# Cross-attention and ternary feed-forward kernel: output product by halves of the rows, value product by pairs of heads, and statistics taken up one step later

## The reference

```
x = x + attention(layernorm(x), ctx)      # x: 64 x 512 x 512, ctx: 64 x 77 x 512
x = x + ffn(layernorm(x))

attention: q = x Wq (16 heads of 32, in 4 groups), k = ctx Wk, v = ctx Wv (4 heads)
    q, k = rope(q), rope(k); sum over the 4 groups of q (the einsum sums over g)
    p = softmax(q k / sqrt(32)) per head over the 77 rows of ctx
    out = mean over heads of (p v); return out @ Wo        # 32 x 512
ffn: w = sign(weight) where |weight| > 0.5 mean|weight|; input quantised by max|x| / 127
    return (round(x / s) @ w.T) * w_scale * s + bias
```

## Time and profile before

| | |
|---|---|
| median of 3 runs | 1268.88 us (1268.54 to 1269.37) |
| the profiled execution | 1268.9 us, its span 1267.0 us |
| TensorE busy, of the span | 1201.2 us, 95% (weight loads 983.0, 78%) |
| VectorE | 1124.7 us, 89% |
| ScalarE | 1001.1 us, 79% |
| GpSimd | 794.2 us, 63% |
| granted TensorE clock, mean | 0.991 |
| DMA | 205 GB/s over the span |

### The profile page before, as it was taken

How to read it: one execution, slowest core, us unless ns; L and a number is a source line. 1 busy time by engine, 2 the same in 40 slices (tenths; PEclk the granted TensorE clock), 3 DMA queues, 4 the chain that set the end, 5 groups by cost and what they waited for, 6 DMA issues and landing times.

```text
span 1267.0 us, 42077 instructions
## 1 busy us (share of the span) xinstructions
PE 1201.2 (95%) x12408; PEld 983.0 (78%) x12471; DVE 1124.7 (89%) x2410; ACT 1001.1 (79%) x2339; POOL 794.2 (63%) x1536
## 2 busy tenths in 40 slices
PE   7999999999999999999999999999789999999997
PEld 7998888888888888888888888888645555555554
DVE  4656999999999999999999999999878888888887
ACT  4566888888888888888888888888768888888886
POOL 4767898898998988989989889899700000000000
PEclk9999999999999999999999999999889999999999
DMA  9772555555555555555555543323029999999945
GB/s 291 225 205 66 160 178 169 173 173 170 164 178 166 178 168 175 170 174 162 182 163 181 164 123 94 87 84 84 2 99 398 403 396 398 399 408 396 395 206 212
DMA packets 97241, 260.26 MB, mean 205 GB/s; under 512 B 42538, under 2 KB 53994, under 8 KB 76723
## 3 DMA queue, kind: packets, MB, share of 16 engines
q1 hardware_dynamic: 97154, 259.75, 59.6%
q10 hardware_dynamic: 48, 0.07, 0.0%
HBM read 137.11 MB, written 122.64 MB: 205 GB/s over the span
## 4 chain that ended last, share of the span: by engine, by line
DVE 44%; PE 35%; issue 15%; DVEq 3%; ACT 1%; POOL 1%; DMA 0%; SPq 0%; POOLq 0%; ACTq 0%
DVE amax L903 10%; PE pT_ps L1265 10%; PE sc_ps L1265 9%; DVE x_sb L940 8%; DVE mx_sb L918 7%; DVE bn_sb L930 6%; DVE e_sb L922 6%; PE qo_ps L1069 5%; PE xT_ps L1256 5%; DVE bn_sb L910 3%; PE sc_ps L1263 2%; DVE mv_sb L947 2%; DVE rinv_sb L890 2%; PE xT_ps L1058 1%; PE pT_ps L1263 1%
## 5 line engine op out<-in xcount | busy, mean ns | idle before, releaser
L1210 PE MATMUL qo_ps<-wqs,xT_sb 128*128 128x128 f32 x2048 | 262.6, 281 | 0.9 <-ACT xT_sb L700 0.9
L1210 PEld LDWEIGHTS qo_ps<-wqs,xT_sb 128*128 128x128 f32 x2048 | 238.2, 191 | 21.5 <-issue 20.0
L1233 PEld LDWEIGHTS pT_ps<-v_blk,pT_sb 103*128 103x128 f32 x1536 | 197.3, 190 | 11.8 <-ACT pT_sb L712 0.9
L940 DVE SCALAR_TENSOR_TENSOR x_sb<-x_sb,mv_sb,xT_ps 128x512 f32 (+1 forms) x256 | 180.0, 745 | 25.5 <-DVE bn_sb L930 10.8
L1233 PE MATMUL pT_ps<-v_blk,pT_sb 103*128 103x136 f32 x1536 | 200.1, 280 | 0.3 <-ACT pT_sb L712 0.3
L1008 DVE TENSOR_TENSOR x_sb<-x_sb 128x512 f32 (+1 forms) x256 | 164.7, 684 | 1.2 <-ACT x_sb L758 1.2
L700 ACT ACTIVATE xT_sb<-xT_ps 128x512 f32<-128x512 f32 x256 | 139.1, 595 | 33.3 <-PE xT_ps L1136 28.9
L663 ACT ACTIVATE sq_sb<-x_sb 128x512 bf16 (+1 forms) x256 | 162.4, 634 | 0.6 <-DVE x_sb L940 0.2
L903 DVE TENSOR_REDUCE amax<-x_sb (+1 forms) x128 | 154.6, 1208 | 0.3 <-issue 0.3
L758 ACT ACTIVATE x_sb<-pT_ps,mean,cols 128x512 f32<-128x512 f32 x128 | 99.5, 777 | 63.6 <-PE pT_ps L1265 63.6
L1265 PE MATMUL pT_ps<-wT,x_sb 128*128 128x512 f16 x512 | 131.4, 379 | 3.2
(11 more groups left out here) (135 smaller groups left out, 2673.7 us busy)
## 6 DMA issues: line engine op xcount, KB each, us to landing
out_y<-x_sb SPq DMA_DIRECT2D x112, 1024.0 KB, 6.5
x_sb<-in_x SPq DMA_DIRECT2D x128, 512.0 KB, 3.9
x_sb<-out_y SPq DMA_DIRECT2D x48, 1024.0 KB, 8.9
x_sb<-in_ctx SPq DMA_DIRECT2D x38, 256.0 KB, 4.0
k_blk<-k_scr SPq DMA_DIRECT2D x256, 9.6 KB, 1.7
v_scr<-x_sb SPq DMA_DIRECT2D x38, 68.0 KB, 3.0
k_scr<-x_sb SPq DMA_DIRECT2D x38, 64.0 KB, 3.3
v_blk<-v_scr SPq DMA_DIRECT2D x128, 10.2 KB
```

Source lines behind the costliest of these rows:

```text
L940: dve.scalar_tensor_tensor(out=x1_at(kj, gj, t), in0=x_sb[:, kj // 2, 2 * (kj % 2) + t, :], scalar=mv_sb[:, kj, t, 0:1], in1=bank[t][:, :] ...
L1210: last = pe.matmul(bank[2][:, t * HD:(t + 1) * HD], xT_sb[:, t, c, :], wqs[:, c, :], start=c == 0, stop=c == EC - 1)
L1233: last = pe.matmul(bank[6][:, t * HEADS * VC:(t + 1) * HEADS * VC], pT_sb[0:CR, t, c * P:(c + 1) * P], v_blk[0:CR, slot, c, :, :].rearrang ...
```

## The change

- **Output product.** GpSimd writes `os_sb` with rounded and rest of each tile once (2 x 64 columns for both tiles instead of 2 x 128). One pair of 64-row transposes turns it: the transposed first tile stands in partitions 0 to 63, the second in 64 to 127. `wst` now holds rounded weights and rest side by side, on all partitions. The product is four matmuls over 64 rows and 512 columns: rounded weights for either tile, then the rest for either tile, accumulated. Each tile has its own bank.
- **Banks.** The output product has a tensor of its own, `y_ps`. q goes to bank 0, where x transposes also go, so these now wait for `q_copied` of the step before. The transposes of q and of `os_sb` go into free columns of the scores' banks and wait for `sub_done_t`; the score matmuls wait for both their copies.
- **Order on TensorE.** The output product stands ahead of q instead of behind it.
- **Chunks.** A transpose of probabilities takes 128 columns (chunks overlap), and the value matmul contracts over 128 rows, but only over the 68 columns of two neighbouring heads, chunk c with heads c and c+1.
- **Statistics.** `bn_sb` has two buffers. `bn_aggr` and the variance of a pair follow a step after its `bn_stats`.
- **Order on the others.** VectorE: see the rows below. ScalarE copies q behind the exponentials. GpSimd puts the two powers between operations that wait for each other.

The core of the diff:

```diff
-STARTS = [c * CR if (c + 1) * CR <= SC else SC - CR for c in range(CHUNKS)]
+STARTS = [min(c * CR, SC - P) for c in range(CHUNKS)]
...
-            then(dve.tensor_copy(wst[:, :], woc[:, :]))
-            then(dve.tensor_tensor(wst[2 * D:4 * D, :], woc[2 * D:4 * D, :],
-                                   wst[2 * D:4 * D, :].bitcast(F32), ALU.subtract))
+            then(dve.tensor_copy(wst[:, 0, :], woc[:, :]))
+            then(dve.tensor_tensor(wst[:, 1, :], woc[:, :], wst[:, 0, :].bitcast(F32), ALU.subtract))
...
-                    pool.tensor_tensor(ost_sb[:, :, :, 0, :],
-                                       pw2_sb[:, :, 0, 0:D].unsqueeze(2).broadcast_to([P, 2, 2, D]),
-                                       pw2_sb[:, :, 1, 0:D].unsqueeze(2).broadcast_to([P, 2, 2, D]),
-                                       ALU.add).then_inc(o_ready, 1)
+                    pool.tensor_tensor(os_sb[:, :, 0, :], pw2_sb[:, :, 0, 0:D], pw2_sb[:, :, 1, 0:D],
+                                       ALU.add).then_inc(o_ready, 1)
...
+                    pool.tensor_tensor(os_sb[:, :, 1, :], o_sb[:, :, 0:D], os_sb[:, :, 0, :].bitcast(F32),
+                                       ALU.subtract).then_inc(os_ready, 1)
...
-                    act.activation(oT_sb[:, :, :].rearrange("p c (h r) -> p c h r", h=2), rows_of(qo_ps, P, 2),
+                    act.activation(oT_sb[:, :].rearrange("p (c h r) -> p c h r", c=1, h=2), rows_of(sc_ps, SC + P, 1),
...
-                    held(ost_ready, j + 1, ost_count, 1)
-                    for t in range(2):
-                        last = halves(qo_ps, P + t * HALF,
-                                      ost_sb[:, t, :, :, :].rearrange("p a b d -> p (a b d)").bitcast(F32))
-                    last.then_inc(oT_done, 1)
+                    held(os_ready, j + 1, o_count, 1)
+                    halves(sc_ps, SC + P, os_sb[:, :, :, :].rearrange("p t a d -> p (t a d)").bitcast(F32))\
+                        .then_inc(oT_done, 1)
...
-                    if isinstance(j, int) and j <= RESID:
-                        at_least(pe, xT_copied_t, 2 * j)
-                    else:
-                        held(added_t, 2 * (j - RESID), added_count, 2)
+                    if not isinstance(j, int) or j > 0:
+                        held(q_copied, j, q_count, 1)
...
-                            last = halves(pT_ps, (t * CHUNKS + c) * HALF, e_sb[:, kj % 2, t, start:start + CR])
+                            last = halves(pT_ps, (t * CHUNKS + c) * HALF, e_sb[:, kj % 2, t, start:start + P])
...
-                    at_least(pe, sub_done_t, 2 * j)
+                    if resid:
+                        pe.wait_ge(oT_copied, resid[0] + 1)
...
+                    for w in range(2):
+                        for t in range(2):
+                            rows = slice(t * HALF, (t + 1) * HALF)
+                            last = pe.matmul(y_ps[:, t, :], oT_sb[rows, :], wst[rows, w, :], start=w == 0, stop=w == 1)
+                    last.then_inc(y_done, 1)
...
-                    for t in range(2):
-                        pe.matmul(bank[t][:, :], oT_sb[:, t, :], wst[:, :], start=True, stop=True)\
-                          .then_inc(y_done_t, 1)
...
-                        for c in range(CHUNKS):
-                            last = pe.matmul(bank[6][:, t * HEADS * VC:(t + 1) * HEADS * VC],
-                                             pT_sb[0:CR, t, c * P:(c + 1) * P],
-                                             v_blk[0:CR, slot, c, :, :].rearrange("p h d -> p (h d)"),
-                                             start=c == 0, stop=c == CHUNKS - 1)
+                        for c in (0, 2, 1):
+
+
+                            at0 = (t * HEADS + c) * VC
+                            last = pe.matmul(bank[6][:, at0:at0 + 2 * VC], pT_sb[:, t, c * P:(c + 1) * P],
+                                             v_blk[:, slot, c, c:c + 2, :].rearrange("p h d -> p (h d)"),
+                                             start=c == 0, stop=c == 1)
```

More of the change, by code:

```diff
@@ L169, in build @@
         wqs = sb("wqs", [P, EC, HD])
-        wst = sb("wst", [P, E], F32R)
+        wst = sb("wst", [P, 2, E], F32R)
         wbar = sb("wbar", [P, D])
@@ L730, in step @@
                                        scale=rs_sb[:, kj, t:t + 1]).then_inc(exp_done_t, 1)
+                if proj:
+                    j, kj, gj = proj
+                    act.wait_ge(q_done, j + 1)
+                    at_least(act, rope_mul, 2 * j)
+                    act.activation(q_sb[:, :], bank[0][:, 0:2 * HD], ACT.Copy).then_inc(q_copied, 1)
                 if stat:
@@ L919, in step @@
                                           AX.X, ALU.max).then_inc(mx_ready, 1)
+                    if rope:
+                        dve.wait_ge(bn_step, 2 * rope[0] + 2)
                     for t in range(2):
@@ L926, in step @@
                                           ALU.subtract).then_inc(sub_done_t, 1)
+                if rope:
+                    j, kj, gj = rope
+                    if not score:
+                        dve.wait_ge(bn_step, 2 * j + 2)
+                    for t in range(2):
+                        dve.bn_aggr(mv_sb[:, kj, t, :], bn_sb[:, kj % 2, t, :]).then_inc(mv_ready, 1)
                 if proj:
                     j, kj, gj = proj
-                    dve.bn_stats(bn_sb[:, 1, :], x_sb[:, kj // 2, 2 * (kj % 2) + 1, :]).then_inc(bn_step, 1)
-                    dve.wait_ge(bn_step, 2 * j + 2)
+                    dve.wait_ge(x_in[kj], gj * 16 + 16)
+                    dve.bn_stats(bn_sb[:, kj % 2, 0, :], x_sb[:, kj // 2, 2 * (kj % 2), :]).then_inc(bn_step, 1)
                 if resid:
@@ L950, in step @@
                        .then_inc(stats_ready, 1)
+                if proj:
+                    j, kj, gj = proj
+                    dve.bn_stats(bn_sb[:, kj % 2, 1, :], x_sb[:, kj // 2, 2 * (kj % 2) + 1, :]).then_inc(bn_step, 1)
             steps(dve, step)
@@ L1148, in step @@
                     for t in range(2):
-                        last = halves(qo_ps, t * HALF, qr_sb[:, kj % 2, t * HD:(t + 1) * HD])
+                        last = halves(sc_ps, SC + t * HALF, qr_sb[:, kj % 2, t * HD:(t + 1) * HD])
                     last.then_inc(qT_done, 1)
```

131 lines of the change are left out of this document (59 added, 72 removed).

## The result

The changed kernel takes 1204.15 us in the median (1203.37 to 1204.22), beside 1268.89 for the kernel before on the same chip: a ratio of 0.9488 (0.9469 to 0.9506). One further execution that took 3110 us is left out. Forecast were 1209.

The account below looks back on a forecast made before the run. No engine stood out, so several needed relief. VectorE's new 5.65 us plus 0.12 waiting and 0.085 loop gave a 5.855 step against 6.345; over 122 steps 59.8 us off 1268.9, forecast 1209, range 1188 to 1246.

Parts of the forecast that it names:

- (a): TensorE: rounded parts of both tiles fill one tile, 2 transposes replace 4; oT falls from 0.13 to 0.07 us.
- (b): TensorE: x transposes wait for the previous step's q_copied, not the residual; the remaining 0.34 of 0.47 us goes.
- (c): TensorE, transposes of probabilities: 12 at 0.033 us each cost 0.39, minus 0.16.
- (d): TensorE, output product: 2 matmuls over 128 rows become 4 over 64; halves overlap, so it stays at 0.55 us.
- rival B: TensorE, output product: the halves do not overlap, 1.10 us; time 1259 to 1274 us; chance 0.06.
- (e): TensorE, weighted values: 12 records half as wide, each needing its weight load of 0.11 us; 1.41 against 1.48.
- rival A: TensorE, value matmuls: weight loads do not hide, 2.0 us instead of 1.41; time 1279 us; chance 0.05.
- it waits for them: VectorE: the 128x2 operation is recorded with 0.51 us because it waits for the two small aggregations.
- The allowance: Step sum: 0.12 us added, between 0 and 0.22, because four engines at 5.3 to 5.65 still hold one another up.
- rival C: Copies before the scores or GpSimd's pw: a new wait eats half the gain; 0.35 us waiting, 1237 us; chance 0.20.
- D: Whole step: no waiting is left and VectorE runs at 5.57 us; step 5.655, time 1185 us; chance 0.09.
- E: VectorE: its 0.70 us stays because it is dispatch of small operations; time 1241 to 1256 us; chance 0.08.

Follow-up runs that it names:

- statistics-only run: The kernel before with only VectorE's new order and statistics taken up a step later: 1223.97 us, ratio 0.9654.

## Why the prediction came out right, and where its reasons did not

**Result and sum.** 1204.15 against 1209; the step 5.761 against 5.855. That is 11.4 us better over 122 steps; run-in and drain took 6.1 that I had put at nothing, part of it with the lower clock shown above. The profiled run, 1204.09, stands at the median.

**TensorE.** (a) 0.12 from the `os_sb` to the x transposes instead of 0.07. (b) The wait is gone, as said; but the statistics-only run shows that the residual's earlier place removes it too, so the bank change was not needed for it. (c) Probabilities 0.49 here, 0.38 in the next step, forecast 0.39: right, and worth nothing in time, as the run with chunks of 103 shows. (d) Output product: scores and product together 0.52 + 0.67 = 1.19, forecast 1.26. Four records in 0.74 of 0.45 each overlap: rival B falls. Undoing the halves was not tried, since the old form's transposes find no free columns in these banks. (e) Values 1.38, forecast 1.41, in place of 1.48: that loads set the pace held, and rival A with 2.0 falls. q takes 1.89, not 1.81; in the waits view its loads wait for the xT copies by 25.4 us in 69 steps. The sum from 504.94 to 510.83 is 5.89, of which 0.13 is the wait for `os_sb`.

**VectorE, the wrong step.** "it waits for them" was wrong. I priced the variance at 0.12; from L953 to the `bn_stats` it is 0.49 and 0.26 in the two steps shown. The operation is blocked by GpSimd, wherever it stands beside a tensor operation of that engine. The 0.22 for `bn_step` did go: from `bn_stats` to the residual 0.58. The other terms held (residual 1.30, `amax` 1.13, `bn_stats` 0.61, subtractions 0.77). What I did not see is the larger effect of the order: it carries 44.7 us by itself and loses 52.4 when undone alone. In the waits views of 400 to 800 us, TensorE's waits for the residual (12.4 us), ScalarE's for the x transposes (13.9) and GpSimd's for the reciprocal (17.7) stand in the kernel before and are gone in the statistics-only run: VectorE's results reach three other engines earlier. I had only counted what it saves on VectorE.

**GpSimd, mis-sized.** I gave it 5.55 and put it third; it takes 5.71 from start to start, and binds together with the variance that it holds up. Its work was right: 377.7 us in flight of 400 are 5.44 per step of 5.761, forecast 5.47. The term that was off is the waits, 0.08 forecast and 0.32 measured in the mean. That "two of its three short waits for itself" go was right, but two others took their place: `rs` behind the blocked variance, and the part sum behind the head sum. "Statistics a step later cost nothing" was wrong too: they cost the first of these, and with the variance early GpSimd has the 5.55 that I gave it. Most of VectorE's steps are then 5.65 to 5.74, near my 5.65; one in eight takes 6.04.

**The allowance** of 0.12 over VectorE's 5.65 happened to cover the 0.06 to GpSimd's 5.71 and the steps of 5.94, a right number for a reason I did not have. This was luck. It is rival C in small, at a place that C did not name.

**The loop.** I split 6.345 into 6.26 and 0.085 for the turning loop. In truth the reciprocals of before are, past the first steps, 6.15 to 6.73 apart in a pattern of eight, so one step was too few to split by; the changed kernel has 5.69 to 5.77 and one of 5.94 to 5.98.

**Rivals D and E.** No waiting at all (5.57) did not come; with the second power left out the step is 5.595, near D's 5.655, but there TensorE ends it and not VectorE, as D had it. E's price, a small operation that stays long, came true for the variance, for another cause and half the size.

## What to carry to other kernels

When all engines are within a few per cent, price an order by when its results reach the other engines, not by what it saves on its own: VectorE's order alone brought two thirds of the gain. Before a tiny VectorE operation is placed, look at what GpSimd runs at that moment: under its long tensor operations it costs up to 0.5 us, under its power operation nothing. And relieve the engine that binds before others: two changes on TensorE (half the columns, wider chunks) shortened their groups by 0.11 and 0.17 and gave no time.

Two versions beat both kernels, each at 1197.3 to 1197.4 us: the change with the variance directly behind the aggregations, or with GpSimd's old order; not both.

## What the hardware showed that I had not expected

- A 128x2 tensor_scalar on VectorE takes 0.12 to 0.17 us free and up to 0.69 when it meets a GpSimd product, sum or difference; all 572 records over 0.25 us end with one. Inside a GpSimd power of 128x2 it takes 0.11 to 0.18.
- A GpSimd power costs 0.70 us for 2 columns and 1.02 for 4, against 0.19 for an addition of 128x2.
- Twelve full-row value records come at 0.115 us each with 68 columns and at 0.124 with 136: the columns hardly count.
- In the run-in of the changed kernel a q group took 3.22 us where the granted clock was 0.50; in the steps it takes 2.05 at 1.00.
